# An expert's weighted sum in a vision tower's FFN: four chained operations on DVE in place of one product and POOL's tree

## The reference

```
h = tokens(x)                         # 64 patches of 28x28x3 per image, times W, plus a class token; times pos_embed
h = h + attention(layernorm(h))       # 8 heads, relu'd q and k, softmax
h = h + ffn(layernorm(h))
# ffn of a token z (128 values):
out_shared = swiglu(z @ shared_in) @ shared_out
g_idx      = argmax of 2 group logits;  top 2 of the 4 experts of that group, weights comb (8 per token, 6 of them zero)
h_expert   = swiglu(z @ expert_in)    # one hidden vector, shared by all experts
routed     = sum over 8 experts e of comb[:, e:e+1] * (h_expert @ expert_out_weight[e].T)
ffn        = out_shared + routed
```

## Time and profile before

| what | value |
|---|---|
| median of 3 runs | 532.13 us (529.61 to 533.96) |
| the profiled execution's own time | 530.89 us |
| its span, first to last instruction | 527.6 us |
| mean granted TensorE clock | 0.944 of full speed |
| PE busy | 481.2 us, 91% |
| DVE busy | 321.8 us, 61% |
| ACT busy | 184.3 us, 35% |
| POOL busy | 173.7 us, 33% |

### The profile page before, as it was taken

One profiled execution on the slowest core, in us unless ns is written; L12 is line 12 of the kernel. 1 busy time (PEld: TensorE's weight loads), 2 busy tenths in 40 slices (PEclk: granted clock), 3 DMA queues, 4 the chain that ended last, 5 costly groups with the idle time before them and its releaser, 6 DMA issues.

```text
span 527.6 us, 7237 instructions
## 1 busy us (share of the span) xinstructions
PE 481.2 (91%) x2322; PEld 323.5 (61%) x2322; DVE 321.8 (61%) x869; ACT 184.3 (35%) x342; POOL 173.7 (33%) x213
## 2 busy tenths in 40 slices
PE   5999997899999999999999999999887878898984
PEld 2355555555775578557755676667666656786562
DVE  0043347375856586747776676757687669646662
ACT  0026214632273217421652256214641464122220
POOL 6012301120462037212821083116421831134353
PEclk9989996999999999999999999999989897969886
DMA  8996560055015600461035300000000000000001
GB/s 336 356 404 216 188 222 24 1 179 187 1 21 155 209 4 2 140 187 61 0 103 166 116 0 20 0 0 1 20 1 0 2 21 1 1 0 2 20 0 22
DMA packets 14413, 44.71 MB, mean 85 GB/s; under 512 B 1721, under 2 KB 7090, under 8 KB 14386
## 3 DMA queue, kind: packets, MB, share of 16 engines
q1 hardware_dynamic: 12882, 42.39, 24.3%
q10 hardware_dynamic: 1504, 1.99, 1.1%
HBM read 42.24 MB, written 2.13 MB: 84 GB/s over the span
## 4 chain that ended last, share of the span: by engine, by line
PE 67%; DVE 15%; issue 7%; DMA 3%; POOL 3%; SPq 3%; ACT 2%; DVEq 0%; POOLq 0%
PE acc L421 22%; PE O L511 5%; PE B L407 4%; PE scores L485 4%; DMA x_main<-in_x_main 3%; DVE z_nat L1083 2%; SPq L385 2%; PE C L623 2%; PE scores L623 2%; PE acc L658 2%; PE B L445 2%; PE C L624 2%; PE C L625 2%; PE B L464 1%; PE C L562 1%
## 5 line engine op out<-in xcount | busy, mean ns | idle before, releaser
L421 PE MATMUL acc<-x_main,w_patch 128*128 128x512 f32 x288 | 140.5, 617 | 6.8 <-DMA w_patch<-in_w_patch 6.0
L421 PEld LDWEIGHTS acc<-x_main,w_patch 128*128 128x128 f32 x288 | 51.6, 195 | 51.9 <-issue 42.0
L1571 POOL TENSOR_TENSOR prod<-prod 128x512 f32<-128x512 f32 (+1 forms) x33 | 42.6, 1292 | 33.7 <-DVE prod L1296 33.7
L511 PEld LDWEIGHTS O<-v_bd,probs_t 128*128 128x128 f32 x256 | 33.0, 197 | 22.2 <-issue 11.2
L842 ACT ACTIVATE probs<-shift 128x512 f32<-128x512 f32 x32 | 20.2, 630 | 73.5 <-DVE shift L1135 73.5
L1564 POOL TENSOR_TENSOR hidden_lo<-silu,hidden_hi 128x512 fp32r<-128x512 f32 (+1 forms) x18 | 20.9, 1162 | 70.2 <-ACT hidden_hi L842 70.1
L511 PE MATMUL O<-v_bd,probs_t 128*128 128x64 f32 (+1 forms) x256 | 35.1, 282 | 4.0 <-ACT probs_t L842 4.0
L1131 DVE TENSOR_REDUCE row_max<-scores 128x8 f32<-128x520 f32 x32 | 22.3, 698 | 21.5 <-PE scores L485 21.3
L842 ACT ACTIVATE probs_t<-B 128x512 f32<-128x512 f32 x32 | 19.0, 594 | 43.7 <-PE B L407 43.2
L1533 POOL TENSOR_TENSOR p_cls<-exp_cls,row_rec 128x16 f32<-128x16 f32 x16 | 3.5, 221 | 91.4 <-DVE row_rec L1151 91.4
L623 PE MATMUL C<-w_eout_hi,hidden_hi 128*128 128x512 f32 (+1 forms) x66 | 31.0, 470 | 1.4 <-POOL hidden_lo L1564 0.7
(11 more groups left out here) (251 smaller groups left out, 1013.2 us busy)
## 6 DMA issues: line engine op xcount, KB each, us to landing
x_main<-in_x_main SPq DMA_DIRECT2D x48, 768.0 KB, 4.3
out_tokens<-y_out SPq DMA_DIRECT2D x16, 128.0 KB, 2.5
w_patch<-in_w_patch ACTq DMA_DIRECT2D x6, 192.0 KB, 9.9
prod<-in_w_eout SPq DMA_DIRECT2D x2, 512.0 KB
x_tail<-in_x_tail SPq DMA_DIRECT2D x8, 96.0 KB, 3.5
silu<-in_w_in SPq DMA_DIRECT2D x2, 256.0 KB
hidden<-in_rows ACTq DMA_DIRECT2D x1, 256.0 KB, 15.6
w_attn<-in_w_attn ACTq DMA_DIRECT2D x1, 256.0 KB, 17.1
```

Source lines behind the costliest of these rows:

```text
L421: last = mm(acc[:, :], w_patch[:, j, :], x_main[:, j, :], start=(j == 0), stop=False)
L511: last = mm(O[:, c:c + 64].rearrange("p (b c) -> p b c", b=2), probs_t[p % 2][:, hp * 128:(hp + 1) * 128], pair, start=True, stop=True)
L1571: q.tensor_tensor(p[r, 0, :], p[r, 0, :], p[r, 1, :], ALU.add).then_inc(tree1_done.sem, 1)
```

## The change

`weigh` no longer writes products. For each of the four experts of its half it issues one scalar_tensor_tensor of 128 columns on DVE: y = (expert's output in PSUM x that token's weight) + y, where the weight is a column of `comb` (one value per partition) and y is the tile's part of `y_out` (or `y_cls`). The eight operations of a tile each wait for the one before, since each reads the y that the last wrote. `expert_sum` on POOL and its calls are gone, as are `output` on DVE and its calls, and `routed` for the class tokens. `prod_done` now counts 32 steps per group instead of 8; PE waits for the same `weigh` calls as before, told in these steps. The wait of `weigh` for POOL's tree is gone; the wait for `shared_add` moved to its first call. The store waits for `prod_done` in place of `yout_done`.

```
-        e_full, prod_done = ev("e_full", 2 * TILES), ev("prod_done", 2 * TILES)
-        tree1_done, tree2_done, tree_done = ev("tree1_done", TILES), ev("tree2_done", TILES), ev("tree_done", TILES)
-        yout_done = ev("yout_done")
+        e_full, prod_done = ev("e_full", 2 * TILES), ev("prod_done", TILES * EXPERTS)
...
             def store(g):
-                need(sp, yout_done, g)
+                need(sp, prod_done, g)
...
-            need(sp, yout_done, GROUPS)
+            need(sp, prod_done, GROUPS, EXPERTS)
...
             def gates(g, tiles, rows):
-                    need(pe, prod_done, g - 1, 5)
+                    need(pe, prod_done, g - 1, 5 * EG)
...
                 elif u >= 4:
-                    need(pe, prod_done, g, u - 3)
+                    need(pe, prod_done, g, (u - 3) * EG)
...
             def weigh(g, u, rows):
                 need(dve, e_full, g, u + 1)
                 if u == 0:
                     need(dve, comb_done, g)
-                if half == 0:
-
-                    if t >= 2:
-                        need(dve, tree_done, g, t - 1)
-                    else:
-                        need(dve, tree_done, g - 1, t + 3)
+                    need(dve, ysh_done, g)
+                y = (y_cls if is_class(g) else y_out)[0:rows, t * D:(t + 1) * D]
                 src = expert_bank(u)
-                v.tensor_tensor(prod[t % 2][0:rows, half, :].rearrange("p (e d) -> p e d", d=D),
-                                src[0:rows, :].rearrange("p (e d) -> p e d", d=D),
-                                bcast(comb[0:rows, t, half * EG:(half + 1) * EG], D), ALU.mult).then_inc(prod_done.sem, 1)
-
-            def output(g, tiles, rows):
-                need(dve, ysh_done, g)
-                need(dve, tree_done, g, tiles)
-                y = y_cls if is_class(g) else y_out
-                v.tensor_tensor(y[0:rows, 0:tiles * D], y[0:rows, 0:tiles * D],
-                                (routed_cls if is_class(g) else routed)[0:rows, 0:tiles].rearrange("p t d -> p (t d)"), ALU.add).then_inc(yout_done.sem, 1)
+                for e in range(EG):
+                    k = half * EG + e
+                    if k:
+                        need(dve, prod_done, g, t * EXPERTS + k)
+                    v.scalar_tensor_tensor(y, src[0:rows, e * D:(e + 1) * D], comb[0:rows, t, k:k + 1], y, ALU.mult, ALU.add)\
+                        .then_inc(prod_done.sem, 1)
...
-            def expert_sum(g, t, rows):
-
-                need(pool, prod_done, g, 2 * t + 2)
-                r, p = slice(0, rows), prod[t % 2]
-                q.tensor_tensor(p[r, 0, :], p[r, 0, :], p[r, 1, :], ALU.add).then_inc(tree1_done.sem, 1)
...
```

More of the change, by code:

```diff
@@ L229, in vit_tower @@
         table_row = sb("table_row", [128, 1])
-        y_cls, routed_cls = x_main[:, 12, 0:D], x_main[:, 12, D:2 * D].rearrange("p (t d) -> p t d", d=D)
+        y_cls = x_main[:, 12, 0:D]
         tc_attn_t = x_main[:, 13, 0:IMAGES]
@@ L1420, in body @@
                     hidden_mul(g - 1, 1, TOK)
-                if last and has_last(g - 1):
-                    output(g - 2, TILES, 128)
                 if last:
@@ L1483, in _ @@
             weights(L, TILES, 128)
-            output(L - 1, TILES, 128)
             shared_add(L, h2[1], TILES, 128)
@@ L1503, in _ @@
             weigh(GROUPS, 1, IMAGES)
-            output(L, TILES, 128)
-            output(GROUPS, 1, IMAGES)
         @block.gpsimd
@@ L1606, in body @@
                 norm_scale2(g, TILES, 128)
-                if last:
-                    for t in range(TILES - 1):
-                        expert_sum(g - 1, t, 128)
                 z_low(g, TOK)
-                if last:
-                    expert_sum(g - 1, TILES - 1, 128)
             groups(pool, body)
@@ L1619, in _ @@
             z_low(GROUPS, IMAGES)
-            expert_sum(L, 0, 128)
-            expert_sum(L, 1, 128)
             hidden_low(GROUPS, 0, IMAGES)
             hidden_low(GROUPS, 1, IMAGES)
-            expert_sum(L, 2, 128)
-            expert_sum(L, 3, 128)
-            expert_sum(GROUPS, 0, IMAGES)
 OUT_SHAPE = (IMAGES, SEQ, D)
```

## The result

The changed kernel takes 548.5 us (median of 4 runs, 548.3 to 550.15) beside 533.05 (4 runs, 529.61 to 535.55) for the kernel before: a ratio of 1.033, 95% interval 1.029 to 1.038. The forecast was 538, +1.1%. The sign and the steps at the joint hold; the loss is three times as large. The profiled execution took 550.15 us, with a span of 548.0, which is 20.4 more than before.

What follows compares the result with a forecast made beforehand. PE was taken to bound the loop, except where it waits for DVE at the joints. Joints +6.6 and +0.1, tail -4.0 and clock +3.4 gave +6.1 on 530.89, 537.0; on the median's scale 538 us, range 525 to 549.

Steps and rivals of the forecast that it cites:

- The sign: Whole kernel: the change makes it slower, 538 us, 1.1% over the median of the kernel before.
- The new operation: DVE in `weigh`: one 128-column operation takes 0.345 us, the next begins 0.377 after it, one `weigh` takes 1.48.
- The slope: DVE's chained operations: some 220 lie on the path, so 0.01 us of pitch is worth 2.2 us.
- Rival A: DVE's chain: operations are cheap; at a pitch of 0.26 the sum is -12.5 us, 520; chance 0.20, at 519 to 532.
- The joint: End of one body and next body's projections: the q addition delays the v projection by 1.32 us, five times, +6.6.
- The sixth: Between the two last bodies, without patch matmuls and already set by DVE: the v projection moves by +0.1 us.
- The tail: From 478 us, one chain through DVE: dearer `weigh` calls against freed routing, store wait and ending, sum -4.0 us.
- the rest of the loop: 0: Loop outside the joint: the removed addition, q normalisation, POOL's queue and SP's stores change nothing, 0 us.
- The clock: PE resting 1.8 us at the joint: the granted clock falls at two of five, +3.4 us.
- The row that argued for two in five: At 482 us: half of the stretch idle, yet PE's clock stayed at 1.00; evidence against a fall everywhere.
- Rival B: Clock falls at every joint, or the pitch is 0.42 or more: 543 to 553 us; chance 0.18.
- Rival C: POOL's z_low and bias addition hold DVE's chained operations at the joint: 12.5 us in all, about 550; chance 0.07.

Runs made afterwards that it cites:

- e7: The changed kernel with the constant 0.5 in place of the weight's pointer, so the weighing is left out: 524.22 us, ratio 0.994 to the kernel before.
- e10: The changed kernel with two accumulators, for even and odd experts, their final addition left out: 518.67 us, ratio 0.974 to the kernel before.
- e2: The changed kernel with its hardware loop written out on all engines but SP: 543.76 us, ratio 1.024 to the kernel before.
- e11: The kernel before with its loop written out on every engine but SP: 532.84 us beside 532.61, ratio 1.000.
- e1: The changed kernel with eight unused matmuls put on PE ahead of the v projection in bodies 2 to 7: 538.93 us, ratio 1.014 to the kernel before.
- e8: The changed kernel with both eight unused PE matmuls ahead of the v projection and the written-out loop: 534.59 us, ratio 1.003 to the kernel before.
- e9: The changed kernel with a group's last `weigh` moved behind the next body's q addition: 537.07 us, ratio 1.012 to the kernel before.
- e5: The kernel before with POOL's trees held until DVE's z_nat scalings are done: 528.64 us, ratio 0.994.

## Why the prediction was right in kind and wrong in size

- **The new operation: right.** 0.345 taken, 0.350 measured; `weigh` 1.48 taken, 1.50 measured (e7 and e10 price its two parts). The Trainium skill (VectorE: DVE Perf Modes, "The DRAIN you can't avoid") has the wait between operations free, by which the chain would have run at 0.26. The trace does not agree: e10 and the changed kernel show 0.26 without and 0.385 with the wait for the operation just before, and the measurement decides.
- **The slope: right.** Rival A said what a pitch of 0.26 would give: 12.5 us faster than before. e10 gave 14 (0.974 of 532.6).
- **The joint: right in its steps, 0.3 us short.** Every step came as written: no wait for z_nat, z_nat in 1.11, then three tiles without a gap, then the q addition. The path from `weigh` 0 to z_nat took 5.39 (5.26 taken) and from z_nat to the v projection 10.88 (10.70). With +1.6 in place of +1.32, the five joints are 8.0 and not 6.6. The sixth cost 1.2 (0.1 taken): PE waits 1.73 us for q there too.
- **The tail: right in sum.** -4.0 taken, -3.4 measured.
- **The loop's back edge: missed.** The step "the rest of the loop: 0" looked at waits and queues, not at the program's length. Two bodies of DVE's loop grew from 198 busy instructions to 248. At the branch DVE sits idle for 2.87 us with nothing to wait for, and one of the page's two instruction queues, q14, has 19 packets where it had 13. One of them moves between 267.0 and 267.5 us, inside the stall, and one at 269.5; the kernel before has none at its back edge (252 to 260 us). The Trainium skill (Runtime: NRT & Kernel Launch, "Instruction fetch mechanics") says that a taken branch to code outside what is held must fetch it first, and the trace agrees: e2 takes the 2.9 us away, and e11 finds none in the kernel before. It falls at the joint, where DVE has no slack to cover it.
- **The clock: the term that failed.** It was put at +3.4, two falls in five joints, and at nothing in body 7. It fell at four of these five (the v projections at 209, 270, 329 and 387 take 2.07 to 2.08 us) and again just behind the sixth (0.73 and 0.50 from 440 to 444 us). In the bodies behind the first three, 4.6 us are left for it. The one at 387 cost nothing on balance: the kernel before already lost 5.2 us of clock in that body (0.90 over 51.9 us), and the changed one loses 4.8 (0.91 over 53.1). In body 7, whose PE already had a clock of 0.85 and which I had left out of the sum, the loss of clock grew by 6.6 us and the kernel lost 6.1. The row that argued for two in five (at 482, half of a stretch idle and the clock at 1.00) is of the tail and was a poor neighbour.

In bodies 2 to 5 the clock's share is e1's finding. For body 7 it is less certain. With a rest of 1.73 us ahead it took 63.26 us, and e1 and e8, with that rest filled, took 58.15 and 54.97. But the kernel before took 57.16 in one profile and, with its loop written out (e11) and no rest ahead either, 60.36 in another, at a clock of 0.80. So some 3 of the 6.1 us can be chance.

The sum of the span then reads: the start -0.7, body 1's fall 1.7, joints 8.0 + 1.2, back edge 2.9, clock in bodies 2 to 5 4.6 (what the 18.4 us from the v projection of body 1 to that of body 7 leave), body 7 6.1, tail -3.4: 20.4, against 6.1 predicted. Of the 14.3 between them, 7.3 are clock (4.6 + 6.1 against 3.4, if all of body 7's is clock), 2.9 the back edge, 2.5 the joints, 1.0 the start and 0.6 the tail. On the medians the loss is 15.5, so 3.8 of the 14.3 are no miss of the forecast.

Rival B (543 to 553, at a chance of 0.18) named the right cause, but its price is partly luck: falls at every joint make 543 by its own term, and the rest came from the back edge and body 7, which it did not have. The forecast's own rest of 1.8 us at the worst place of each group should have carried it higher. Rival C is excluded: the chained operations are 350 ns everywhere, beside POOL's h_nat and z_low too.

What stays open is which part of body 7's loss is due to the rest before it and which is chance.

## What to carry to other kernels

Price a chain of dependent operations by its pitch, and split the accumulator in two before giving up on it: here that alone, with the two sums left apart, turned +3.3% into -2.6%, and the whole version, with the addition and two smaller edits, reached -2.9%. Put work that nobody waits for behind the operation that another engine waits for, not ahead of it. And when a change lets TensorE rest at a point where it never did, count the rest at least twice: once for itself, once for the half clock that can follow.

## What the runs showed of the hardware

- A wait for the operation just before costs a 128-column DVE operation 0.125 us of pitch (0.385 against 0.26); with a wait for the one before that, the pitch is 0.26, that of unwaited scalings of this size.
- The scalar's pointer costs 0.06 us per operation (350 ns with it, 290 with a constant).
- The granted clock and PE's rest at a joint: after rests of 0.51 to 0.78 us (e7, five joints) the v projection ran at full clock (1.16 us) each time. After 1.58 to 1.73 (the changed kernel, five joints) it took 2.07 or 2.08, the 1.2 GHz level, three times and 1.16 twice; after one of these two (440) the clock fell right behind it, after the other (152) it stayed at 1.00. After 2.14, 2.83, 3.39 and 4.59 (e10, e9, e7 and the changed kernel at the back edge) it took 2.08. The exception is e1's back edge: a rest of 2.43 right behind eight matmuls of 512 columns, and 1.16.
- POOL's tree of operations stretches DVE's four z_nat scalings from 1.11 to 2.92 us (e5), while a product read from PSUM stays at 0.68 beside a tree (309.50 to 310.18, the tree's first step from 309.06 to 310.35 us).
- A loop of two bodies with 248 DVE operations stalls DVE for 2.87 us at its back edge; with 198 there is no such stall (the changed kernel and the kernel before).
